# Guard keys of a unit: four ScalarE copies with a factor per partition in place of one GpSimd product

## What is computed

```python
Q, K, V = (proj(Wq, bq), proj(Wk, bk), proj(Wv, bv))
Kg = K[:, :, idx]
Vg = V[:, :, idx]
s_scores = jnp.einsum('bhsd,bhskd->bhsk', Q, Kg) * scale
s_scores = jnp.where(prior_index_mask[:Ss][None, None], s_scores, -jnp.inf)
sparse_out = jnp.einsum('bhsk,bhskd->bhsd', jax.nn.softmax(s_scores, axis=-1), Vg)
x = x + ffn0(sparse_out @ Wo.T + bo)      # 256 -> 1024 -> 256, relu
x = x + ffn1(cond1(x))                    # 256 -> 1024 -> 256, gelu; 8 experts of 256 x 256, top 2
```

## Time and profile before

| what | value |
|---|---|
| median of 3 executions | 569.64 us |
| the profiled execution | 570.82 us |
| its span, first to last instruction | 568.40 us |
| TensorE busy | 521.5 us (92%) |
| VectorE busy | 408.6 us (72%) |
| ScalarE busy | 225.7 us (40%) |
| GpSimd busy | 84.2 us (15%) |
| mean granted TensorE clock | 0.98 |

### The profile page before, as it was taken

One profiled execution on the slowest core, in us unless ns is written; L12 is line 12 of the kernel. 1 busy time (PEld: TensorE's weight loads), 2 busy tenths in 40 slices (PEclk: granted clock), 3 DMA queues, 4 the chain that ended last, 5 costly groups with the idle time before them and its releaser, 6 DMA issues.

```text
span 568.4 us, 7403 instructions
## 1 busy us (share of the span) xinstructions
PE 521.5 (92%) x2649; PEld 360.3 (63%) x2649; DVE 408.6 (72%) x788; ACT 225.7 (40%) x381; POOL 84.2 (15%) x94
## 2 busy tenths in 40 slices
PE   3897888999899999889969999999999999999896
PEld 1454445454454445436748887888878888788775
DVE  4887879878887777845867598483884839847295
ACT  4204476667665656764526240042400415003100
POOL 3002544315133120300141000010000100000000
PEclk9999699999999999999999999999999999999999
DMA  7200011101010000000451000100001000010000
GB/s 250 57 2 0 1 37 38 37 2 38 1 39 1 1 0 2 1 1 0 114 146 38 1 1 20 46 10 0 2 18 47 11 2 0 20 46 2 9 12 31
DMA packets 11756, 15.37 MB, mean 27 GB/s; under 512 B 5954, under 2 KB 8258, under 8 KB 11714
## 3 DMA queue, kind: packets, MB, share of 16 engines
q1 hardware_dynamic: 11714, 14.83, 8.5%
HBM read 12.73 MB, written 2.10 MB: 26 GB/s over the span
## 4 chain that ended last, share of the span: by engine, by line
PE 39%; DVE 6%; POOL 2%; issue 1%; DMA 1%; ACT 1%; SPq 0%; DVEq 0%; POOLq 0%
PE psG L1546 4%; PE psG L1545 4%; PE psG L1544 4%; PE psM L1544 3%; PE psM L1545 3%; PE psM L1546 3%; PE psS L1544 3%; PE psS L1545 3%; PE psS L1546 3%; PE psO L1544 3%; PE psO L1546 3%; PE psO L1545 3%; DVE hT_lo L1694 1%; DVE hT_hi L1692 1%; DMA staged<-ew_dram 1%
## 5 line engine op out<-in xcount | busy, mean ns | idle before, releaser
L737 DVE TENSOR_REDUCE few_Qa<-psG 128x2 fp32r<-128x512 f32 x116 | 74.7, 686 | 28.5 <-PE psG L506 28.4
L657 ACT ACTIVATE Pr<-psS 128x512 f32<-128x512 f32 x128 | 71.4, 599 | 28.5 <-PE psS L528 19.5
L744 DVE SCALAR_TENSOR_TENSOR Pr<-Pr,few_W 128x1024 f32<-128x1024 f32 x48 | 72.8, 1520 | 10.2 <-ACT Pr L657 10.1
L524 PE MATMUL psS<-few_QAT,few_KP 128*128 128x512 f32 x128 | 52.9, 457 | 10.5 <-ACT Pr L657 9.8
L504 PE MATMUL psG<-few_KG,QG 128*128 128x512 f32 x116 | 53.0, 515 | 2.9 <-DVE few_Qa L737 2.9
L1655 ACT ACTIVATE V<-psS,cols 128x512 f32<-128x512 f32 x16 | 11.0, 690 | 103.3 <-PE psS L1546 102.6
L1694 DVE TENSOR_TENSOR hT_lo<-V,hT_hi 128x512 fp32r<-128x512 f32 x64 | 46.5, 726 | 2.2
L506 PE MATMUL psG<-Mneg,few_identb 128*128 128x512 bf16 x116 | 46.8, 403 | 0.0
L524 PEld LDWEIGHTS psS<-few_QAT,few_KP 128*128 128x128 f32 x128 | 22.3, 188 | 38.2 <-issue 30.7
L1692 DVE CAST hT_hi<-V 128x512 fp32r<-128x512 f32 x64 | 34.2, 535 | 12.7 <-ACT V L1655 6.2
L540 PE MATMUL psO<-Pr,few_VA 128*17 128x512 f32 x256 | 33.5, 598 | 0.0
(11 more groups left out here) (251 smaller groups left out, 1194.7 us busy)
## 6 DMA issues: line engine op xcount, KB each, us to landing
Pr<-xT_dram SPq DMA_DIRECT2D x2, 1024.0 KB, 8.6
staged<-w_dram SPq DMA_DIRECT2D x4, 512.0 KB, 3.7
x1T<-xT_dram SPq DMA_DIRECT2D x4, 512.0 KB, 4.2
staged<-ew_dram SPq DMA_DIRECT2D x4, 512.0 KB, 4.0
out_dram<-y SPq DMA_DIRECT2D x16, 128.0 KB, 1.7
staged<-fc_dram SPq DMA_DIRECT2D x2, 512.0 KB, 3.8
Pr<-wqkv_dram SPq DMA_DIRECT2D x1, 768.0 KB, 4.9
staged<-fc2a_dram SPq DMA_DIRECT2D x1, 512.0 KB, 3.4
```

Of the source, the lines that this page charges most:

```text
L524: mm = nc.tensor.matmul(psS[:, f, :], self.KP[:, u % 2, j, r * P:r * P + P], self.QAT[:, u % 2, j // 2, q], start=True, stop=not logged)
L657: nc.scalar.activation(Pr[:, i % JOBS, 512 * f:512 * f + 512], psS[:, f, :], ACT.Exp, scale=SCALE).then_inc(self.s["s_exp"], 1)
L737: nc.vector.tensor_reduce(self.Qa[:, f % SLOTS, st, 2 * p:2 * p + 2, 48], self.guard_bank(i)[0][:, p, :].rearrange("p (h t) -> p h t", h=2 ...
L744: nc.vector.scalar_tensor_tensor(pr, pr, FMAX, self.W[:, r, :], ALU.min, ALU.mult).then_inc(self.s["s_prob"], 1)
```

## The change

GpSimd's product is gone; in ScalarE's stream, at the same step and behind the copies of QG and KT, stand four activations of the function Copy, one per head, each over 128 partitions x 256 keys with the head's mask column as scale. The last one signals kg_ready. The two waits (kt_out, g_scores) move with it.

```diff
@@ GpSimd's stream
-                    if what == "guard_keys":
-                        pool.wait_ge(self.s["kt_out"], i // 2 + 1)
-                        if i >= 2:
-                            pool.wait_ge(self.s["g_scores"], 2 * JOBS * (i - 1))
-                        hm = headmask[:, HG * (i % 2):HG * (i % 2) + HG]
-                        nc.gpsimd.tensor_tensor(
-                            self.KG[:, i % 2, :, :],
-                            self.KT[:, None, :].to_broadcast([P, HG, FEW_KEYS]),
-                            hm[:, :, None].to_broadcast([P, HG, FEW_KEYS]), ALU.mult).then_inc(self.s["kg_ready"], 1)
@@ ScalarE's stream
                         nc.scalar.copy(self.KT[:, :], self.misc_bank("kt_out", i // 2)[:, 0:FEW_KEYS]).then_inc(self.s["kt_out"], 1)
+                    if what == "guard_keys":
+                        act.wait_ge(self.s["kt_out"], i // 2 + 1)
+                        if i >= 2:
+                            act.wait_ge(self.s["g_scores"], 2 * JOBS * (i - 1))
+                        for h in range(HG):
+                            mm = nc.scalar.activation(self.KG[:, i % 2, h, :], self.KT[:, :], ACT.Copy,
+                                                      scale=headmask[:, HG * (i % 2) + h:HG * (i % 2) + h + 1])
+                        mm.then_inc(self.s["kg_ready"], 1)
```

## The result

| | before | changed |
|---|---|---|
| median | 569.64 us (5 executions) | 574.21 us (5 executions: 573.39 to 575.79) |
| ratio | | 1.0083, interval 1.0068 to 1.0099 |
| profiled execution | 570.82 us | 574.08 us |
| its span | 568.40 us | 572.3 us |
| VectorE busy | 408.6 us | 402.2 us |

What follows compares the result with a forecast made beforehand. Bound: a chain hopping between engines, TensorE waiting for ScalarE at unit boundaries, not busy shares. Sum: 1.56 x 3 + 0.39 + 0.12 + 1.15 - 0.08 = 6.26 us, giving 575.9 us; range 573.7 to 579, with rival 1 573.0 to 579.2.

Steps and rivals of the forecast that it cites:

- The price of a place: Four added ScalarE copies where no gap covers them: 1.46 us, or 1.56 where KT's copy stands just in front.
- the pitch: Start to start of the added ScalarE copies, back to back: 0.365 us taken, bounds 0.30 and 0.50.
- The added wait for KT: Units 0, 2, 4 and 6: ScalarE waits for its own copy of KT, +0.10 us each.
- Relief at units 5 and 7: VectorE weighings beside the removed GpSimd product fall from 2.56 to 1.22 us, a gain of 1.34 us each.
- Unit 6: Between KT and an exponential: 1.56 us less 0.41 absorbed by a wait for TensorE, +1.15.
- Unit 0: Opening, between KT's copy and first query rows: full 1.56 us, plus 0.39 for transposes at the low clock.
- Unit 1: Before the first transposed query rows: copies hidden in 4.15 us idle; GpSimd freed earlier, 0 to 0.3, taken 0.
- Unit 2: Before the table load and first exponentials, no ScalarE gap up to TensorE's waits at 80.87 and 83.88: +1.56 us.
- rival 2: Clock falls a second time, at unit 2, costing 1.5 to 3.5 us; total +8 to +10, 578.8 us; chance 0.10.
- 1 (VectorE takes up half of the boundaries): VectorE's stretched weighings absorb half of three full prices, 2.3 us: +3.9, 573.6 us; chance 0.15.
- 3 (the copies hide at units 2, 4 and 6): Copies hidden everywhere but the opening: -0.7 us; with the opening hidden too -2.68, 567.0 us, chance 0.03.
- Rival 4: Scaled copy needs another function table, loads of 1.28 us around the copies: +13 to +16, about 590 us; chance 0.03.

Runs made afterwards that it cites:

- experiment 2: Kernel before, with the keys of units 3, 5 and 7 made by ScalarE one step earlier than in the changed kernel: ratio 0.9948, 566.40 us beside 569.29.
- experiment 3: Kernel before, with keys on ScalarE for units 2, 4 and 6 alone: 1.0073, 573.78 us; for unit 0 alone: 1.0029, 570.85 us.
- experiment 1: Kernel before, with GpSimd's products of units 3, 5 and 7 made later, same engine and size: ratio 0.9965, 567.39 us beside 569.29.
- experiment 7: Kernel before, with keys of units 1, 3, 5 and 7 from ScalarE in its idle time, even units on GpSimd: ratio 0.9908, 564.42 us.
- experiment 4: Kernel before, with ten unread matmuls ahead of the counts' transposes: 1.0011; also unit 1 alone on ScalarE: 0.9972; units 0 and 1: 0.9997.

## Why the prediction was right, and where not

- **The bound** (boundaries where TensorE waits for ScalarE, not the busy shares): right. Experiments 2 and 3 show it from both sides.
- **The price of a place**, forecast 1.56 and 1.46 us: measured 1.74 and 1.61. The term that was small is the pitch, 0.365 taken and 0.40 measured. I had scaled a 128x512 row down by the slope of plain copies; the estimate from the Trainium skill ("ScalarE: Activation LUTs", What ACT_TABLE_LOAD costs), 0.49 us each and 0.40 apart, which I had set beside the sum, is what the trace shows (0.496 and 0.40).
- **The added wait for KT**: 0.10 forecast, 0.13 seen (1.74 - 1.61). Right.
- **Relief at units 5 and 7**, 1.34 us each: right in place and mechanism (experiment 1); in the ledger they net +0.23 and -0.10, forecast +0.12 and -0.08. Cover at units 1 and 3: right.
- **Unit 6**: 1.15 forecast, 1.19 in the ledger.
- **Unit 0**: forecast 1.95, measured 1.6 alone and 1.72 between the QG copies. The 0.39 of it that I gave to the clock is not there: I had let the fall of the clock stay at its old moment, and it came later too (at 55.9 in the changed kernel and 55.5 with unit 0 alone, where it had been 54.5). The first transposes of the changed kernel, at 54.91, still took 0.62 us. The size was right where the clock did fall ahead of them (0.40 to 0.42 in the profiles of both units together and of experiment 7).
- **Unit 1: the step that failed.** "At unit 1 GpSimd is freed a little earlier for splitting keys, worth 0 to 0.3 us; I take 0." It is worth 1.5 (0.96 to 1.84 us between the QG copies in the four profiles with unit 1's keys on ScalarE; the two least, 0.96 and 1.38, are those whose first transposes ran at the low clock). I had looked for who waited for GpSimd in the profile of before and found no such wait of size; it was covered by a low clock that differs from one execution to the next. The row that could have told me is GpSimd's own timeline from 63.1 to 72: no gap, the product in the middle.
- **Unit 2**: 1.56 forecast, 1.80 at the high clock, 2.24 in the profile. The rest goes beside rival 2, whose low stretch I had given a chance of 0.10 and a price of 1.5 to 3.5 us. It came, which the prediction had named as a sign of being wrong, but at 0.4 us: the exponentials were 3.31 us late at 90.19, and only 1.71 at 95.77. Before, TensorE had stood 1.35 us at 90.49 for VectorE, behind a weighing stretched to 3.18 us (86.56); after, that weighing took 2.23 (88.69) beside slow guards, and the wait is gone. With unit 2 alone and the clock high, both are there as before (3.19 and 1.35). Most of the low clock's price fell into a wait that was there anyway.
- **The rest**: 0.55 us less outside the span, below, which no step had.

With what was measured, the sum of the prices taken alone is 1.6 - 1.5 + 4.5 (units 2, 4, 6) + 0.1 (units 5 and 7 by the ledger) = 4.7 us, where 4.6 was measured. That it fits so well is in part luck, since each of the three medians has its own loss of time outside the span in it; by the spans the sum is 1.85 - 1.35 + 4.95 + 0.1 = 5.6, where 5.3 was measured. Stage by stage the ledger leads from the forecast to the result: 6.26 - 2.07 (units 0 and 1) + 0.68 (units 2 and 3) + 0.17 + 0.11 + 0.04 - 0.02 (units 4 to 7) = 5.17, less 0.55 outside the span.

So the range held by a partial cancellation: about 2 us too much for the opening and 0.55 outside the span, against nearly 1 us too little at the other places. The range itself was added up too narrow: the forecast with the pitch of 0.50 and the clock's 1 us is 580.3, not 579. The result lies at its other end.

Of the rivals, 1 (VectorE takes up half of the boundaries) and 3 (the copies hide at units 2, 4 and 6) are refuted by experiment 3, where these three cost 1.86, 1.77 and 1.24. For units 5 and 7 experiment 2 shows that hiding can be had, by moving the copies one step. Rival 4 is out: no table load stands at a copy.

The 0.84 us that the dense layers give back in the profiled pair are most likely not the change's. From the last OTs to the end the 13 profiles take 300.9 to 302.8 us, and before has the longest of all, 1.2 us more than the same layers in experiment 4's kernel with the added matmuls. The two profiles have their low stretches at other places there (296.8 to 300.2 before, over the matmuls with Wo; 291.4 to 298.2 after, ahead of them; and the last 1.9 us of the span before against 1.0 after). The median spans, 567.0 us in 18 executions of before and 572.3 in 5 of the changed kernel, are 5.3 apart, as the ledger was at the end of the attention (4.74 + 0.41 = 5.15).

## What to carry to other kernels

Price moved work by the place where it lands: read the engine's gap right there and the gaps behind it up to the first wait of somebody else, and forget its busy share. Read the side effect of what is removed in the neighbour's durations, and see if a mere shift in time would bring it without changing engines. When a trace has a stretch at a low clock, ask of each engine whether its own stream is gapless in it: a second limit may lie just beneath. Then removing what the trace blames wins nothing by itself, while taking work off the hidden path can win.

## What the runs showed of the hardware

- A factor per partition in place of a number makes a 128x256 activation 496 ns long in place of 402, also back to back (four in 1.70 us in place of 1.34).
- The time outside the span (execution less span) is, by medians, 2.28 to 2.38 us in the kernel before, with matmuls added to it and with the product only shifted, 2.15 to 2.17 with unit 1 or unit 2 on ScalarE alone, 2.05 with unit 0 alone, 1.96 with units 0 and 1, and 1.79 to 1.87 with three or more units there. Nothing in the traces explains it; it makes 0.5 us of the difference between experiments 1 and 2.
- TensorE's low clock in the opening lasted 13.6 us in the profile of before; in the kernel of experiment 1, with the same opening, it came in two shorter stretches (54.8 to 58.2 and 61.7 to 65.1). The QG copies were 27.65 us apart in the first and 27.66 in the second: a clock that varies from one execution to the next can cost nothing, when another engine ends last.
